# Starting GpSimd's two row sums at the release of their rows instead of after the norm product z

## What is computed

```python
# layer 0: group norm, then channel attention from the 256x256 Gram matrix
v = gn(x); a = v.reshape(b, h*w, c)
attn = softmax(einsum('bpi,bpj->bij', a, a))
x = x + gamma * einsum('bpc,bcj->bpj', a, attn) + v
# layer 1: group norm, then box sums at four scales
v = gn(x); v = (v - v.min(per image)) / (v.max(per image) - v.min(per image) + EPS)
log_m = log(stack([box(v, k) for k in (2, 4, 8, 16)]) + EPS)
alphas = slope of log_m against log k
excite = sigmoid(relu(mean(alphas) @ w1 + b1) @ w2 + b2)
sim = cosine between log_m and its fitted line, both centred over the scales
x = x + sim * sigmoid(batch_norm(alphas)) + (1 - sim) * v * excite
```

## Time and profile before

| what | value |
|---|---|
| time, median of 2 runs (range) | 7062.98 us (7059.15 to 7066.81) |
| the profiled execution's own time | 7073.4 us |
| its span, first to last instruction | 7071.6 us |
| mean granted clock of TensorE | 0.886 of full speed |
| busy: DVE, PE, ACT, POOL | 82%, 74%, 69%, 22% |

### The profile page before, as it was taken

The page is one execution under the profiler, slowest core; times in us unless marked ns, Lnnn a source line. Parts: engine busy times, 40 slices in busy tenths (PEclk is TensorE's granted clock), DMA queues, the critical chain, the costliest instruction groups (busy, mean ns, idle before and its releaser), DMA issues. The chain is left out here.

```text
span 7071.6 us, 107841 instructions
## 1 busy us (share of the span) xinstructions
PE 5245.1 (74%) x35320; PEld 4754.5 (67%) x35320; DVE 5823.8 (82%) x6709; ACT 4867.7 (69%) x5203; POOL 1535.4 (22%) x945
## 2 busy tenths in 40 slices
PE   7968885888858887688858888588876777466643
PEld 6767775777757776677757777577765666466642
DVE  1359997899969998699978999699987999699971
ACT  0128885788848877588857888488875888588861
POOL 0022222222132211321222212221213212322210
PEclk9989997999979998899979999799987999788875
DMA  3634443556535655465545655365653555344446
GB/s 114 195 116 152 145 142 122 176 196 211 190 128 201 204 190 174 147 211 196 199 146 169 203 201 199 118 204 194 207 175 128 187 175 176 124 149 150 152 149 231
DMA packets 837653, 1210.47 MB, mean 171 GB/s; under 512 B 34608, under 2 KB 690000, under 8 KB 821072
## 3 DMA queue, kind: packets, MB, share of 16 engines
q1 hardware_dynamic: 837456, 1208.16, 50.8%
HBM read 671.16 MB, written 536.87 MB: 171 GB/s over the span
## 5 line engine op out<-in xcount | busy, mean ns | idle before, releaser
L384 POOL TENSOR_TENSOR t<-t 128x1024 f32<-128x1024 f32 (+3 forms) x800 | 1340.0, 1688 | 4325.4 <-DVE logs L962 4282.8
L516 PE MATMUL even<-band,t 128*128 128x128 f32 x12288 | 1866.2, 283 | 459.6 <-ACT logs L692 286.5
L516 PEld LDWEIGHTS even<-band,t 128*128 128x128 f32 x12288 | 1618.5, 196 | 543.2 <-issue 443.0
L497 PE MATMUL h_ps<-mix,xt 128*128 128x256 f32 x4096 | 1206.9, 447 | 603.2 <-DVE mx L877 562.9
L497 PEld LDWEIGHTS h_ps<-mix,xt 128*128 128x128 f32 x4096 | 865.1, 222 | 785.5 <-issue 519.2
L692 ACT ACTIVATE logs<-even,col 128x1024 f32<-128x1024 f32 x512 | 569.1, 1111 | 430.8 <-PE even L516 430.1
L877 DVE CUSTOM_DVE_ANT_0 h_out<-h_ps,shift,mx 128x512 f32<-128x512 f32 x512 | 382.7, 747 | 574.2 <-PE h_ps L497 574.1
L518 PE MATMUL even<-band,t 128*128 128x128 f32 x4096 | 791.9, 275 | 0.0
L474 PE MATMUL g_ps<-xa 128*128 128x257 f32 x2048 | 623.8, 386 | 41.6 <-DMA xa<-in_x_dram 41.6
L533 PE MATMUL o_ps<-ident,pd 128*128 128x128 f32 x2048 | 386.6, 321 | 318.8 <-ACT o_sb L746 176.3
L518 PEld LDWEIGHTS even<-band,t 128*128 128x128 f32 x4096 | 621.9, 192 | 0.0
(11 more groups left out here) (184 smaller groups left out, 10433.0 us busy)
## 6 DMA issues: line engine op xcount, KB each, us to landing
xa<-in_x_dram SPq DMA_DIRECT2D x256, 512.0 KB, 5.4
xb<-in_x_dram SPq DMA_DIRECT2D x256, 512.0 KB, 6.2
h_scratch<-h_out SPq DMA_DIRECT2D x128, 1024.0 KB, 4.1
hr<-h_scratch SPq DMA_DIRECT2D x256, 512.0 KB, 5.8
p_scratch<-x1t SPq DMA_DIRECT2D x256, 512.0 KB, 2.7
q_scratch<-ut SPq DMA_DIRECT2D x256, 512.0 KB, 4.1
pd<-p_scratch SPq DMA_DIRECT2D x256, 512.0 KB, 6.1
qd<-q_scratch SPq DMA_DIRECT2D x256, 512.0 KB, 6.9
```

The lines of the kernel that those rows point to most:

```text
L384: ins = g.tensor_tensor(dst[:, hf, d:d + n, :], src[:, hf, d:d + n, :], src[:, hf, e:e + n, :], ALU.add)
L497: ins = t.matmul(h_ps[:, r * C:(r + 1) * C], xt[:, q % 2, jh, r, :], mix[:, jh, :], start=(jh == 0), stop=(jh == 1))
L516: ins = t.matmul(o, src[:, hf, at, :], band[:, which, :], start=True, stop=(which < 3))
```

## The change

In POOL's `half_chunk` the first wait is another one. Before, POOL waits until z of unit u-1 is made (L962, in DVE's half chunk u). Now it waits until the high contrast of unit u-1 is made (L931, in DVE's half chunk u-1), which says that PE's last reads of the rows to be replaced are over. The wait for `t_ready[2]` in `more_row_sums` stands as before behind it.

```diff
                     def half_chunk(i, k, hf):

                         u = 32 * image + 4 * i + 2 * k + hf
-                        pool.wait_ge(z_ready, u)
+                        pool.wait_ge(d23_ready, u + 1)
                         more_row_sums(1 - k if hf == 1 else k, 1 - hf, u + 4 + 2 * image)
```

## The result

| | before | after |
|---|---|---|
| time, median (range) | 7062.98 us (7059.15 to 7066.81) | 7976.66 us (7976.42 to 7976.91) |
| ratio | | 1.1289, 95% interval 1.1262 to 1.1317 |
| span of the profiled execution | 7071.6 us | 7975.2 us |
| mean granted clock of TensorE | 0.886 | 0.841 |

What follows compares the result with a forecast made beforehand. DVE, 82% busy, was taken as the bound. POOL's sums holding DVE (833 us), less 45 for turn 9's collisions, plus 97 for PE's later mix, made +885 us: 7948 us at the median, range 7740 to 8150.

Steps and rivals of the forecast that it cites:

- Where POOL starts: POOL's row sums would start behind DVE's L913 instead of L962, about 5 us earlier.
- The order at the start: DVE's L892, issued 0.08 us before L913 ends, would come first; POOL, some 0.2 us behind L913, would meet it.
- the upper bound's case: POOL comes ahead of L892: 0.2 us more in 240 calls, 0.96 more in 112 small calls, +156 us.
- The price of a meeting: A DVE instruction with all inputs in SBUF, held by a POOL sum, loses the sum's length less 0.32 us.
- The number of meetings: POOL's sums hold DVE twice in 128 large calls, three times in 98 small ones, turn 2 less: 833 us.
- the lower bound: POOL may not get in between L892 and L957; 98 small calls then lose 0.96 us less each, -94 us.
- Given back: Turn 9's collisions of POOL's sums with DVE's L939 and L941 go: 45 us less.
- What is late next: PE's mix, behind the first L877, comes later at a low clock; DVE's hole ahead of the second L877 grows, 97 us.
- the case's own range: The forecast's case, given 80%, runs from 7757 to 8150 us.
- POOL never gets in: DVE's L892 to L962 keep POOL out until L877, so DVE loses nothing: 7063 us; 5%.
- Part is absorbed: The hole ahead of DVE's second L877 swallows some delay and 97 us of low clock don't come: 7665 us; 7%.
- PE becomes a bound as well: PE's low clock lasts beyond the mix, slowing transposes and box matmuls, 326 us on top: 8274 us; 8%.

Runs made afterwards that it cites:

- the delay alone: The kernel before with two more row reductions on DVE ahead of L957, some 3.5 us a unit, and no early sums: 8062.8 us, ratio 1.142.

## Why the prediction was right, step by step

- **Where POOL starts.** Right: released by L913 in 224 waits and by the count of the zero rows in 16, about 5 us sooner in the unit. The name in the diff, `d23_ready`, releases nobody.
- **The order at the start.** Right in all but 10 units. In the two units an image with zero rows, the count comes by DVE's queue and not with an instruction's end, and there POOL can be first. In turns 3 to 7 it is, in both units of each. DVE there, and POOL there:

```profile
2155.37 3.41 DVE L892 SCALAR_TENSOR_TENSOR pd<-qd,col,pd 128x1024 f32<-128x1024 f32 x1 [0.16 <-DVE t L902]
2158.70 3.36 DVE L957 TENSOR_TENSOR logs<-logs 128x1024 f32<-128x1024 f32 x1
2162.10 1.23 DVE L960 TENSOR_TENSOR logs<-logs 128x1024 f32<-128x1024 f32 x1
```

```profile
2155.34 5.64 POOL L384 TENSOR_TENSOR t<-t 128x1024 f32<-128x1024 f32 x2 [17.74 <-DVEq L905]
```

  POOL is issued 0.03 us ahead of L892, and it is L892 that is held. In turns 8 and 9 the same piece of code comes out the other way, with POOL 0.07 us behind:

```profile
6879.67 1.28 DVE L892 SCALAR_TENSOR_TENSOR pd<-qd,col,pd 128x1024 f32<-128x1024 f32 x1 [0.16 <-DVE t L902]
```

```profile
6879.74 6.71 POOL L384 TENSOR_TENSOR t<-t 128x1024 f32<-128x1024 f32 x2 [17.62 <-DVEq L905]
```

  The first order is the upper bound's case. Ten such units at 2.0 to 2.1 us make 21 of L892's 23 us; the rest comes from the first L892 of some images, beside POOL's sums at the image's start. It costs next to nothing in all, since in these units L892 and L957 are held and L960 (1.23 us) is not. It is also the rule of the Trainium skill (SBUF — State Buffer, "Who interferes with whom") that issue order decides who blocks; this trace shows both orders.
- **The price of a meeting.** Named as the sum's length less 0.32 us. Measured in the two units that the section on the result shows: L957 lost 2.17 us to a sum of 2.37 and L960 2.03; with small sums 0.53, 1.51 and 0.95 us for 0.73, 1.82 and 1.28. So less 0.32 holds where DVE's instruction waits for the one ahead of it (L960, L962), and less 0.20 at L957. L957 is issued back to back behind L892 and so may stand held for longer; that reason is argued, not tested. The 0.12 us more at L957 in 210 meetings make 25 us, and the four lines grew by 852 us and not 833: this term was 2% too small. The whole length of a sum would have made 1018 us. So of the Trainium skill's rule (SBUF — State Buffer, "SBUF: two separate sides", where it is stated for an instruction with two SBUF inputs) its "fully blocks" holds, and its "for the whole instruction" is 0.2 to 0.3 us too much if it is read as the recorded length of a sum. The records don't show whether the ports are free in that time or the record is longer than the hold.
- **The number of meetings.** Right. POOL gets in between L892 and L957, so the lower bound fell, and in the small calls the fourth sum lies beside L877, which stays at 0.74 us. In turn 2, without L892, L957 isn't held, and L960 and L962 are.
- **Given back.** 45 us named, 44 measured (L939 means 1.228 us and L941 1.225 over all turns).
- **What is late next.** 97 us named, 104 measured as L877's whole wait, but this nearness is partly luck. Summed over the timelines, the hole ahead of the second L877 in turns 2 to 8 grew from 201 to 322 us, by 121: it stands at 1.5 us a unit and not at 1.36, which was the hole of one unit and no ceiling (in the kernel before it goes from nothing to 1.6 us). Against that the wait of each image's first copy, 2.2 to 2.4 us, is gone, 16 us in seven images, where the prediction named nothing. That the growth belongs to any delay of DVE and not to the meetings was argued then and is shown by the delay alone (102 us).
- **The total.** 885 us named, 904 measured between the spans and 914 between the medians; the time is 7977 us where 7948 was named, inside the case's own range.
- **The rivals.** POOL never gets in: excluded by the trace of after. Part is absorbed: excluded by the delay alone. PE becomes a bound as well: excluded, since L925 and L931 don't wait for ACT any more than before (L925 26.1 us after 29.8, L931 1.1 in both).

## What to carry to other kernels

A wait can be worth its idle time for what it keeps an engine from colliding with. Before you let GpSimd start sooner, list what VectorE runs in that window and how many of its inputs are in SBUF. Here the same sums cost VectorE nothing beside instructions that read PSUM or one tensor, and nearly their whole length beside those that read two. Look first at the idle holes of the bounding engine: moving an instruction that was ready into one gave 169 us here, while the earlier start of an engine at 22% had nothing to give.

## What the runs showed that I had not expected

- Two engines that meet take strict turns however short the sums are: L957 (1.75 us), L960 (2.73) and L962 (2.17) are held by one sum each, in order, and all 98 units of this kind in turns 3 to 9 show the same three lengths within 0.1 us.
- The held time is booked as busy time on both engines. DVE's share rose from 82% to 83% while it did no more work; only the mean of a line against its like (2742 ns against 1225) tells.
- A tenth of a microsecond decides who is held. L892 took 1.28 us with POOL issued 0.07 us behind it, and 3.41 us with POOL issued 0.03 us ahead.
